# Graph network on one core: the edge-count matrix built from strips of 16 nodes with fp32 keys, in place of 32 nodes with 16-bit keys

## What is computed

```python
x = _layernorm(x + _L0_gnn_ref(x, edge_attr_64, src, dst, ...), axis=-1)
x = _layernorm(x + _L1_gnn_ref(x, edge_index, edge_weight, ...), axis=-1)
x = _layernorm(x + _L2_gnn_ref(x, edge_weight1, ..., src, dst), axis=-1)
x = _layernorm(x + _L3_gnn_ref(x, ..., src, dst), axis=-1)
```

## Time and profile before

| | us |
|---|---|
| median of 3 runs (lowest and highest) | 3524.32 (3522.18 to 3537.60) |
| the profiled execution, its own time | 3527.64 |
| its span, from the first to the last instruction | 3525.7 |
| busy: PE, PEld | 2560.2, 1985.6 |
| busy: DVE, POOL, ACT | 1970.7, 1737.9, 682.7 |
| mean granted TensorE clock, as a share of full speed | 0.852 |

### The profile page before, as it was taken

The page is one execution under the profiler, slowest core; times in us unless marked ns, Lnnn a source line. Parts: engine busy times, 40 slices in busy tenths (PEclk is TensorE's granted clock), DMA queues, the critical chain, the costliest instruction groups (busy, mean ns, idle before and its releaser), DMA issues.

```text
span 3525.7 us, 64349 instructions
## 1 busy us (share of the span) xinstructions
PE 2560.2 (73%) x18318; PEld 1985.6 (56%) x18422; DVE 1970.7 (56%) x6179; ACT 682.7 (19%) x1571; POOL 1737.9 (49%) x1779
## 2 busy tenths in 40 slices
PE   7566767666765565556767676577777699999997
PEld 6344334434435555554555555456665478888775
DVE  3477777676756555556667676667767621111222
ACT  3223333333330000001111111011111231111110
POOL 0554444444407777776777776677777500000000
PEclk9788887787766878787889888798889889999998
DMA  5876555565503333333333343333333322332221
GB/s 187 246 208 175 173 173 170 164 179 166 170 20 101 109 110 111 109 110 95 114 120 115 117 123 97 91 116 115 118 112 113 97 79 98 103 102 93 88 96 58
DMA packets 185480, 435.80 MB, mean 124 GB/s; under 512 B 42835, under 2 KB 89161, under 8 KB 185417
## 3 DMA queue, kind: packets, MB, share of 16 engines
q0 software_dynamic: 93184, 272.74, 26.7%
q1 hardware_dynamic: 88634, 159.04, 13.9%
q10 hardware_dynamic: 3600, 3.28, 0.3%
HBM read 390.37 MB, written 44.51 MB: 123 GB/s over the span
## 4 chain that ended last, share of the span: by engine, by line
PE 31%; POOL 26%; issue 21%; DVE 13%; DMA 6%; ACT 2%; SPq 1%; DVEq 1%; POOLq 0%; ACTq 0%
POOL gath L767 25%; PE banks L1411 15%; DVE prod L1752 3%; PE banks L1256 3%; DMA gath<-h_table,idx_slot 3%; PE banks L1239 2%; PE banks L1170 2%; DVE rh L1756 2%; DVE gath L1780 2%; DVE rh L1780 2%; PE banks L1303 1%; PE banks L1227 1%; DMA misc<-counts 1%; PE banks L1080 1%; PE banks L1242 1%
## 5 line engine op out<-in xcount | busy, mean ns | idle before, releaser
L767 POOL DMA_INDIRECT gath<-h_table,idx_slot x1248 | 1293.2, 1036 | 371.3 <-issue 344.5
L1256 PE MATMUL banks<-onehot,gath 128*128 128x128 f32 x4992 | 782.6, 323 | 479.8 <-DMA gath<-h_table,idx_slot 451.6
L1256 PEld LDWEIGHTS banks<-onehot,gath 128*128 128x128 f32 x4992 | 730.8, 233 | 538.0 <-DMA gath<-h_table,idx_slot 452.2
L1411 PE MATMUL banks<-gath,misc 128*128 128x256 bf16 x1875 | 516.5, 275 | 0.0
L1411 PE MATMUL banks<-acc,misc 128*128 128x256 bf16 x2500 | 421.4, 277 | 23.4 <-DMA misc<-counts 14.5
L765 POOL DMA_INDIRECT rh<-kv_table,idx_slot x208 | 211.1, 1015 | 215.3 <-PE banks L1230 163.1
L765 POOL DMA_INDIRECT gath<-kv_table,idx_slot x208 | 209.0, 1005 | 214.0 <-PE banks L1230 159.7
L1314 PE MATMUL banks<-gath 128*128 128x512 bf16 x624 | 243.7, 414 | 64.7 <-DVE gath L1958 64.7
L1411 PEld LDWEIGHTS banks<-acc,misc 128*128 128x128 bf16 x2500 | 243.4, 99 | 70.3 <-issue 16.8
L1958 DVE TENSOR_SCALAR gath<-w_qkv 128x800 bf16<-128x800 f16 x728 | 257.5, 424 | 0.0
L1838 DVE TENSOR_TENSOR acc<-acc,banks 128x256 f32 x156 | 65.3, 418 | 339.0 <-PE banks L1256 327.2
(11 more groups left out here) (217 smaller groups left out, 3552.4 us busy)
## 6 DMA issues: line engine op xcount, KB each, us to landing
misc<-counts SPq DMA_DIRECT2D x75, 800.0 KB, 4.3
counts<-misc SPq DMA_DIRECT2D x26, 800.0 KB, 3.9
gath<-h_table,idx_slot POOLq DMA_INDIRECT x1248
rh<-in_dst_rows SPq DMA_DIRECT2D x106, 128.0 KB
w_qkv<-in_ef_t SPq DMA_DIRECT2D x106, 128.0 KB
q_win<-q_table SPq DMA_DIRECT2D x208, 64.0 KB
rh<-mask_dram SPq DMA_DIRECT2D x424, 8.0 KB
kv_table<-onehot SPq DMA_DIRECT2D x25, 256.0 KB, 2.0
```

The lines of the kernel that those rows point to most:

```text
L767: pool.indirect_dma_start(row_slot[:, k, t, :], None, source, row_index).then_inc(gath_done[k][t // HALF], 16)
L1256: last = nc.tensor.matmul(banks[:, 3 * k + c, 0:P], row_slot[:, k, t, c * P:(c + 1) * P], onehot[:, k, t, :], start=(t == 0), stop=(t == T ...
L1411: last = nc.tensor.matmul(banks[:, slot, 0:D], c_slot[:, slot, c, :], parts[n % 2][j][:, c, :], start=(c == 0 and j == 0), stop=(c == NB - ...
```

## The change

Strips become 16 nodes (`KW`) wide. A group now builds two of them, of at most four tiles each (`ST` = 4), each with its own first tile and its own PSUM bank. A key has 400 values in place of 800 (`SC` = 25 times 16), and `key_iota` is fp32 in place of fp16. The number of destination nodes per group is 32 as before, and so are the layout and the number of the stores. The input checks, the constants and the table of first tiles are doubled to fit. Line numbers below are those of the hunks, cut to their core:

```diff
@@ -43,13 +43,13 @@
-ST = 7
+KW = SW // 2
+ST = 4
-SC = NB * SW
+SC = NB * KW
-SPLIT_BANK = 512 // SW
@@ -113,11 +113,13 @@
-        tile0_i = sb("tile0_i", [1, P], I32)
+        tile0_i = sb("tile0_i", [1, 2 * P], I32)
+        strip_at = sb("strip_at", [P, 2])
+        first_tile = sb("first_tile", [P, 2])
@@ -159,7 +161,8 @@
-        key_iota = w_qkv_t[:, 2 * NT:2 * NT + SC // 2].bitcast(F16)
+        key_iota = w_qkv_t[:, 2 * NT:2 * NT + SC]
+        strip_no = w_qkv_t[:, 1300 + 2 * TG:1300 + 2 * TG + 2 * STRIPS]
@@ -199,8 +202,8 @@
-        oh_key = upper[:, 0:ST * SC // 2].bitcast(BF16).rearrange("p (t n) -> p t n", t=ST)
-        oh_src = upper[:, ST * SC // 2:ST * SC // 2 + ST * P // 2].bitcast(BF16).rearrange("p (t n) -> p t n", t=ST)
+        oh_key = upper[:, 0:ST * SC].bitcast(BF16).rearrange("p (t n) -> p t n", t=2 * ST)
+        oh_src = upper[:, ST * SC:ST * SC + ST * P].bitcast(BF16).rearrange("p (t n) -> p t n", t=2 * ST)
@@ -233,6 +236,7 @@
+        STRIP_BANKS = (2, 5)
@@ -946,10 +950,10 @@
-                    nc.scalar.activation(c_build[:, 0:SPLIT_BANK, bass.ds(at, SW)],
-                                         banks[:, 2, :].rearrange("p (c n) -> p c n", n=SW), ACT.Copy)
-                    nc.scalar.activation(c_build[:, SPLIT_BANK:NB, bass.ds(at, SW)],
-                                         banks[:, 5, 0:SC - 512].rearrange("p (c n) -> p c n", n=SW), ACT.Copy).then_inc(strip_out, 1)
+                    for j, bank in enumerate(STRIP_BANKS):
+                        last = nc.scalar.activation(c_build[:, :, bass.ds(at + j * KW, KW)],
+                                                    banks[:, bank, 0:SC].rearrange("p (c n) -> p c n", n=KW), ACT.Copy)
+                    last.then_inc(strip_out, 1)
@@ -1310,10 +1315,10 @@
-                    for t in range(ST):
-                        nc.tensor.matmul(banks[:, 2, :], oh_src[:, t, :], oh_key[:, t, 0:512], start=(t == 0), stop=(t == ST - 1))
-                        last = nc.tensor.matmul(banks[:, 5, 0:SC - 512], oh_src[:, t, :], oh_key[:, t, 512:SC],
-                                                start=(t == 0), stop=(t == ST - 1))
+                    for j, bank in enumerate(STRIP_BANKS):
+                        for t in range(ST):
+                            last = nc.tensor.matmul(banks[:, bank, 0:SC], oh_src[:, j * ST + t, :], oh_key[:, j * ST + t, :],
+                                                    start=(t == 0), stop=(t == ST - 1))
@@ -1498,10 +1503,12 @@
...
+            for c in range(2):
+                link(nc.vector.tensor_scalar(last_lt, last_i, strip_at[:, c:c + 1], None, ALU.is_lt))
+                link(nc.vector.tensor_reduce(first_tile[:, c:c + 1], last_lt, AX.X, ALU.add))
...
@@ -1512,12 +1519,13 @@
...
+            link(V.tensor_scalar(strip_at[:, :], strip_at[:, :], float(KW), None, ALU.add))
+            for c in range(2):
+                link(V.tensor_scalar(check, first_i, strip_at[:, c:c + 1], None, ALU.is_lt))
...
@@ -1946,15 +1954,18 @@
-                    tile0 = dve.value_load(tile0_i[0:1, bass.ds(s, 1)], min_val=0, max_val=NT - ST)
+                    tile0 = [dve.value_load(tile0_i[0:1, bass.ds(s * 2 + j, 1)], min_val=0, max_val=NT - ST) for j in range(2)]
-                    V.scalar_tensor_tensor(key_tile[:, k, 0:ST], dstrip[:, bass.ds(tile0, ST)], iota_f[:, bass.ds(s, 1)],
-                                           key1[:, bass.ds(tile0, ST)], ALU.is_equal, ALU.mult).then_inc(key_done, 1)
-                    for t in range(ST):
-                        V.tensor_scalar(oh_src[:, t, :], iota_f[:, :], src_lo[:, bass.ds(tile0 + t, 1)], None, ALU.is_equal)
+                    for j in range(2):
+                        last = V.scalar_tensor_tensor(key_tile[:, k, j * ST:(j + 1) * ST], dstrip[:, bass.ds(tile0[j], ST)],
+                                                      strip_no[:, bass.ds(s * 2 + j, 1)], key1[:, bass.ds(tile0[j], ST)], ALU.is_equal, ALU.mult)
+                    last.then_inc(key_done, 1)
+                    for j in range(2):
+                        for t in range(ST):
+                            V.tensor_scalar(oh_src[:, j * ST + t, :], iota_f[:, :], src_lo[:, bass.ds(tile0[j] + t, 1)], None, ALU.is_equal)
-                    for t in range(ST):
+                    for t in range(2 * ST):
@@ -2012,17 +2023,19 @@
-                        V.tensor_scalar(lo, dst_i[:, :], SW - 1, None, ALU.bitwise_and)
-                        link(V.tensor_scalar(hi, dst_i[:, :], 5, None, ALU.arith_shift_right))
+                        V.tensor_scalar(lo, dst_i[:, :], KW - 1, None, ALU.bitwise_and)
+                        link(V.tensor_scalar(hi, dst_i[:, :], 4, None, ALU.arith_shift_right))
-                        link(V.scalar_tensor_tensor(key1, src_hi[:, :], float(SW), key1, ALU.mult, ALU.add))
+                        link(V.scalar_tensor_tensor(key1, src_hi[:, :], float(KW), key1, ALU.mult, ALU.add))
+                        V.tensor_copy(strip_no[:, 0:P], iota_f[:, :])
+                        link(V.tensor_scalar(strip_no[:, P:2 * STRIPS], iota_f[:, 0:2 * STRIPS - P], float(P), None, ALU.add))
```

More of the change, by code:

```diff
@@ L1512, in count_broken @@
                 link(V.tensor_tensor(broken[:, 0:1], broken[:, 0:1], broken[:, 1:2], ALU.add))
-            link(V.tensor_copy(broken[:, 0:1], part_i[:, :]))
-            link(V.tensor_scalar(broken[:, 0:1], broken[:, 0:1], float(SW), float(SW), ALU.mult, ALU.add))
-            link(V.tensor_scalar(check, first_i, broken[:, 0:1], None, ALU.is_lt))
-            link(V.tensor_reduce(broken[:, 0:1], check, AX.X, ALU.add))
-            link(V.tensor_tensor(broken[:, 0:1], broken[:, 0:1], part_f[:, :], ALU.subtract))
-            link(V.tensor_scalar(broken[:, 0:1], broken[:, 0:1], float(ST), None, ALU.is_gt))
+            link(V.tensor_scalar(strip_at[:, :], strip_at[:, :], float(KW), None, ALU.add))
+            for c in range(2):
+                link(V.tensor_scalar(check, first_i, strip_at[:, c:c + 1], None, ALU.is_lt))
+                link(V.tensor_reduce(broken[:, c:c + 1], check, AX.X, ALU.add))
+            link(V.tensor_tensor(broken[:, :], broken[:, :], first_tile[:, :], ALU.subtract))
+            link(V.tensor_scalar(broken[:, :], broken[:, :], float(ST), None, ALU.is_gt))
+            link(V.tensor_tensor(broken[:, 0:1], broken[:, 0:1], broken[:, 1:2], ALU.add))
             count_broken(PJ, lambda c: V.tensor_tensor(c, run_i, prev_i, ALU.is_lt))
@@ L1547, in _ @@
             dve.wait_ge(pe_small, 1)
-            link(nc.vector.tensor_copy(tile0_i[:, :], banks[0:1, 7, 0:P]))
-            link(nc.vector.tensor_reduce(path_f[:, :], banks[0:1, 7, P:2 * P], AX.X, ALU.add))
+            link(nc.vector.tensor_copy(tile0_i[:, :], banks[0:1, 7, 0:2 * P]))
+            link(nc.vector.tensor_reduce(path_f[:, :], banks[0:1, 7, 2 * P:3 * P], AX.X, ALU.add))
             nc.vector.tensor_scalar(path_i[:, :], path_f[:, :], 0.5, None, ALU.is_lt).then_inc(path_known, 1)
```

11 lines of the change are left out of this document (5 added, 6 removed).

## The result

The changed kernel takes 3484.69 us (median of 4 runs, 3481.33 to 3488.4) against 3524.89 us of the kernel before in the same session (3522.18 to 3537.6). The ratio is 0.9879, 95% interval 0.9853 to 0.9905: **faster by 1.2%**. The forecast was 3541 us with a range from 3495 to 3589, and a chance of 0.17 for faster. It was wrong, in direction too.

The account below looks back on a forecast made before the run. POOL's gather issue, slowed by gathers held during DVE's comparison runs, was taken to bound the strip stages. +18.5 us for the eighth comparison and -2.2 us at stage ends gave +16.3: 3541 us, range 3495 to 3589.

Parts of the forecast that it names:

- What bounds the stages: Second and third grouped stage: POOL's gather pace sets their length; strips cost only gathers held by DVE's key comparisons, 100.5 us.
- The comparison and the run: DVE's key comparisons (L1958): 400 fp32 columns take 0.41 us each, eight in a row 2.78 us.
- The number of caught runs: Comparison runs on DVE that hold a POOL gather until they end: still 47 of 104, forecast range 35 to 60.
- fewer gathers are caught: Rival: DVE's later start and PE's shorter strip shift the meetings with gathers; 3495 us at 25 caught, chance 0.13.
- random starts give 47 again, give or take 5: Argument against fewer caught runs: randomly placed comparison runs would catch about as many of the 104 as before.
- The eighth comparison: One more key comparison per strip on DVE lengthens each run by 0.34 us and costs POOL +18.5 us together.
- a longer run also catches a few more gathers: Part of the extra comparison's cost: some seven of 104 gathers more, each for half of 0.34 us, +1.1 us.
- The rest of DVE's strip: Extra key instruction, register load, source one-hot and comparison add about 0.85 us a strip, hidden in DVE's waits: 0.
- I am wrong if POOL waits for PE: Sign against the forecast: POOL's gathers in the strip stages having to wait for PE's groups, where none was expected.
- the matmuls cost nothing in the loop: PE's strip gets 1.1 us shorter, but inside the loop POOL waits for nothing that depends on it: 0.
- PE's strips at 1.45 us: PE's matmuls per strip, scaled by columns from 2.53 us for 5600 to 3200 columns.
- The ends: Ends of the second and third stage, where the last strip lies on the path: 2 x -1.1 = -2.2 us.

Follow-up runs that it names:

- e9: The kernel before with source one-hots and key comparisons of a strip taking turns on DVE, instead of seven after seven; ratio 0.9870 to the kernel before.
- e5: The kernel before with PE's strip shortened to 3,192 columns (some keys left out of the counts), DVE's work unchanged; ratio 1.0058.
- e6: The kernel before with one more key instruction, source one-hot and key comparison per strip on DVE, into unused memory; ratio 1.0157.
- e7: The changed kernel with PE's strip back at 5,600 columns through extra matmuls with a zero stationary operand; ratio 1.0077 to the kernel before.
- e3: The kernel before with an eighth key comparison of 800 fp16 columns per strip, written where nobody reads; ratio 1.0055.
- e4: The changed kernel with source one-hots and key comparisons taking turns on DVE instead of eight after eight; ratio 0.9919 to the kernel before.

## Why the prediction was wrong

**What bounds the stages: right.** Held-up gathers set the two stages' length, not PE's work. The stages lost 47.5 us while the gathers' busy time fell by 49.2; e9 shows it from the other side. (The remark that no gap was ever ended by another engine is too strong: the profile puts 15 of them down to PE, but they are no longer than the others, 0.31 us.)

**The comparison and the run: right.** 0.41 us was taken, the median is 0.417; a run is 2.79 us in the median, 2.78 was forecast; the longest gather has 3.65 us against 3.5. A caught run loses 2.27 us, where the forecast had 1.92 + 0.34 = 2.26.

**The number of caught runs: this step failed.** "I take today's share because the new run has the same length of comparison and the same gaps between them as the old": 47 of 104 became 15, outside the 35 to 60 that the forecast covered. With the prediction's own terms, 15 x 2.27 + 89 x 0.2 = 52 us of loss stands against 100.5, and 48 us is the gain of the two stages. The rival "fewer gathers are caught" (3495 us at 25 caught, chance 0.13) is what happened, beyond its own example. The reason that it gave, DVE starting later, PE's strip being shorter and the comparisons meeting POOL's rhythm elsewhere, is not what the runs bear out: neither of the first two carried the count from one group to the other (43 in e5, 50 in e6, 26 in e7), and at the same meeting fewer are held. What lowers the count stays open. Its chance was too low because I treated the count as a draw that the change would repeat, "random starts give 47 again, give or take 5". Executions of one kernel do differ by some such width: those of the kernel before lie up to 44 us apart in one session (3494.02 to 3538.31), some 20 caught runs' worth. But the share itself goes with the kernel, as far as one trace of each can tell, and nothing that I read in the trace of before predicts it: among kernels whose runs are all 2.44 to 2.79 us long it went from 11 to 64 of 104.

**The eighth comparison: right as a term.** e3 measured about 19 us against 18.5 (7 to 31 by the interval), but beside a count that fell by 32 it was the small term. One part of it, +1.1 us because "a longer run also catches a few more gathers", has the mechanism wrong: no gather that started over 1.0 us into a run was ever held, so a longer run has no more chances, and e3 has 46 caught for 47.

**The rest of DVE's strip: mis-sized.** It was priced at 0.85 us (its own terms, 0.23, 0.21 and 0.34, make 0.78) and costs about 1.3. From the first key instruction to the last comparison a strip takes 4.78 us in the median for 3.98, which is as forecast. But DVE stands idle ahead of it for 0.65 us on average, 0.16 before, because of the second register load, which the prediction names and doesn't price. The room was also measured at the wrong place: 6.45 us is that of the fifth gather, and the first had 4.80. Nearly all of the 1.3 us still stayed hidden, but the room was used up and POOL waited for PE in five gathers, 2.6 us in all. "I am wrong if POOL waits for PE" came true in that small measure. That the matmuls cost nothing in the loop holds in the kernel before (e5) and not in the changed one (e7).

**PE's strips: half right.** "PE's strips at 1.45 us" holds where PE had been at work; 42 of 104 took over 2.8 us, at the lower clock. The prediction scaled one strip at full clock and took the lower clock to touch only the ends of the stages.

**The ends: right.** The last strip of the second stage takes 1.52 us on PE (before 2.53), and the two stage ends came out 1.4 and 2.1 us shorter, for 1.1 each.

## What to carry to other kernels

Where POOL issues gathers one after the other, look at the maximum of the gather's duration before anything else: here a median of 0.95 and a maximum over 3 us were gathers held by DVE, and POOL's whole pace paid for them. Don't put long comparisons back to back on DVE beside such a stream; a short instruction between any two brought the old kernel as much as the whole change. It makes DVE's series 0.3 us longer, though, and in the changed kernel, where DVE had no room left, it brought nothing more (e4). And a share that one trace shows of how often two engines collide is not a constant to multiply with: the range has to hold a very different share on both sides.

## What the hardware showed that I had not expected

- The hold depends on what is back to back, not on DVE's load. Series of 128-wide fp32 comparisons never held a gather beyond 1.07 us; runs of 400 fp32, 800 16-bit and 400 16-bit columns held one to the end of the run; the same long ones with a 0.27 us comparison between them held none beyond 1.49. A run of 2 to 2.8 us held a gather only if that had started within 1.0 us of the run's first comparison (608 of 608). By the Trainium skill (SBUF — State Buffer, "Who interferes with whom") the lock is one instruction long; the trace agrees for the mixed series and not for the plain runs.
- A register load for a dynamic address took 0.30 us on DVE's sequencer, with 0.19 us of register work behind it. The second one left DVE idle for about 0.5 us more a strip, the largest single part of what the narrower strips cost it.
- A strip of 3,200 columns took PE 1.53 us at a granted clock of 1.00 and 2.85 us at 0.50, the latter where PE had just stood idle for DVE. Less work on PE so came back only in part: 74 us of its busy time where the columns promised 126.
